# Single layer norms of a 16-sublayer kernel, rewritten: wide variance, Ln and Exp in place of Sqrt and reciprocal

## What is computed

```python
def _layernorm(x, axis=-1, eps=1e-05):
    m = jnp.mean(x, axis=axis, keepdims=True)
    v = jnp.var(x, axis=axis, keepdims=True)
    return (x - m) / jnp.sqrt(v + eps)
...
x = x + sublayer(_layernorm(x, axis=-1), weights)
```

## Time and profile before

| what | value |
| --- | --- |
| median of 3 runs | 3856.74 us (3844.39 to 3859.89) |
| the profiled execution | 3816.58 us, span 3814.8 us |
| TensorE (PE) busy | 3021.5 us, 79% |
| DVE (VectorE) busy | 2024.3 us, 53% |
| ACT (ScalarE) busy | 1374.9 us, 36% |
| GpSimd (POOL) busy | 670.1 us, 18% |
| mean granted TensorE clock | 0.864 |

### The profile page before, as it was taken

One profiled execution on the slowest core, in us unless ns is written; L12 is line 12 of the kernel. 1 busy time (PEld: TensorE's weight loads), 2 busy tenths in 40 slices (PEclk: granted clock), 3 DMA queues, 4 the chain that ended last, 5 costly groups with the idle time before them and its releaser, 6 DMA issues. The chain is left out here.

```text
span 3814.8 us, 57392 instructions
## 1 busy us (share of the span) xinstructions
PE 3021.5 (79%) x22522; PEld 1598.0 (42%) x22522; DVE 2024.3 (53%) x3730; ACT 1374.9 (36%) x2632; POOL 670.1 (18%) x561
## 2 busy tenths in 40 slices
PE   6566877788887699897688889977878658867986
PEld 4454247323475244444222224422233443654555
DVE  5211254588753788203788771166763453536643
ACT  3211434623243366423567762210102112223652
POOL 0000017065354100004443200000000000240003
PEclk9666869788888799999899999978789679977997
DMA  2022002022012321000311000000000000023202
GB/s 103 14 66 63 0 19 56 16 94 66 17 47 80 72 40 28 1 0 13 66 30 29 2 1 0 10 0 0 0 0 0 1 0 21 25 56 77 48 15 67
DMA packets 81292, 118.55 MB, mean 31 GB/s; under 512 B 12743, under 2 KB 51623, under 8 KB 79763
## 3 DMA queue, kind: packets, MB, share of 16 engines
q1 hardware_dynamic: 74003, 100.67, 10.6%
q0 software_dynamic: 7040, 14.43, 1.4%
HBM read 90.04 MB, written 24.81 MB: 30 GB/s over the span
## 5 line engine op out<-in xcount | busy, mean ns | idle before, releaser
L1674 DVE TENSOR_REDUCE at_mp<-PS 128x1 f32<-128x384 f32 (+3 forms) x640 | 313.3, 538 | 115.3 <-PE PS L1524 99.0
L1624 ACT ACTIVATE at_pt<-PS 128x384 f32<-128x384 f32 (+3 forms) x704 | 288.4, 456 | 212.8 <-PE PS L1536 177.6
L1521 PE MATMUL PS<-at_kx,at_qx 72*128 72x384 bf16 (+5 forms) x640 | 218.4, 346 | 67.7 <-DMA at_kx<-L_attn_a_parts 26.7
L1534 PE MATMUL PS<-at_qx,at_kx 105*128 105x512 bf16 (+5 forms) x704 | 214.8, 315 | 8.0 <-ACT at_pt L1624 6.0
L3860 ACT ACTIVATE ls_pt<-PS,ls_far 128x512 f32<-128x512 f32 x256 | 155.4, 684 | 23.1 <-PE PS L3681 18.6
L4007 DVE CUSTOM_DVE_ANT_0 PS<-PS,ls_pt 128x1024 f32<-128x1024 f32 x128 | 153.8, 1240 | 18.1 <-ACT ls_pt L3860 15.1
L2287 DVE TENSOR_TENSOR_SCAN mb_ring<-PS,mb_ring 128x1024 f32<-128x1024 f32 x64 | 146.6, 2291 | 18.9 <-POOL mb_ring L2226 6.7
L2242 PE MATMUL PS<-mb_ring,ident 128*128 128x512 f32 x256 | 147.7, 729 | 6.0 <-DVE mb_ring L2292 6.0
L1536 PE MATMUL PS<-at_above,identb 128*128 128x128 bf16 x704 | 134.1, 223 | 0.0
L2271 ACT ACTIVATE PS<-mb_dt,mb_a 128x1024 f32<-128x1024 f32 x64 | 71.6, 1118 | 168.1 <-DVE mb_ring L2287 168.1
L1521 PEld LDWEIGHTS PS<-at_kx,at_qx 102*128 102x128 bf16 (+1 forms) x640 | 64.5, 101 | 161.3 <-DVE at_mp L1674 85.6
(11 more groups left out here) (820 smaller groups left out, 6787.0 us busy)
## 6 DMA issues: line engine op xcount, KB each, us to landing
dl_arena<-in_fir_bank SPq DMA_DIRECT2D x32, 256.0 KB, 3.2
lnA<-mb_rows SPq DMA_DIRECT2D x16, 512.0 KB, 3.7
XN<-mb_rows SPq DMA_DIRECT2D x16, 512.0 KB, 3.7
ffn_place<-in_ffn_L SPq DMA_DIRECT2D x4, 1152.0 KB, 17.2
at_qx<-L_attn_a_parts SPq DMA_DIRECT2D x24, 192.0 KB
at_kx<-L_attn_a_parts SPq DMA_DIRECT2D x72, 64.0 KB
at_qx<-L_attn_b_parts SPq DMA_DIRECT2D x24, 192.0 KB
at_kx<-L_attn_b_parts SPq DMA_DIRECT2D x72, 64.0 KB
```

What stands on the lines that cost most here:

```text
L1521: mm = nc.tensor.matmul(PS[:, n % 3, 0:e - c], QX[0:RAW, u % 3, g, blk(i, P)], KX[0:RAW, u % 3, g, c:e], start=True, stop=True)
L1534: mm = nc.tensor.matmul(PS[:, 3 + n % 3, 0:e - c], KX[0:FULL, u % 3, g, blk(j, P)], QX[0:FULL, u % 3, g, c:e], start=True, stop=True)
L1624: nc.scalar.activation(PT[:, y % SLOTS, g, 0:e - c], PS[:, 3 + n % 3, 0:e - c], ACT.Exp, scale=SCALE).then_inc(exp_done, 1)
L1674: nc.vector.tensor_reduce(best, sc, AX.X, ALU.max).then_inc(s_maxed, 1)
```

## The change

The norm keeps each token's values on all partitions throughout. TensorE multiplies x by `center_mat` (identity less 1/128), which gives x less its mean straight into PSUM. ACT squares from PSUM into `lnA`. The variance product now has `mean_mat` stationary and 512 columns of squares moving, so every partition holds the variance. ACT takes Ln of variance plus eps, then Exp of minus a half times that, both 128x512, in place in `lnA` (`rstd` is now `lnA`). DVE does one product a block, from PSUM and `lnA` into `XN`. The narrow tile `rstd` is gone, and `center_mat` (64 KB) is built on GpSimd. The semaphores `mean_ready`, `std_ready`, `rstd_ready` and `spread_ready` go, `log_done` and `root_done` come.

```diff
-    sq, rstd = k.lnA, k.rstd
+    sq, rstd = k.lnA, k.lnA
...
         @block.tensor
         def _(pe):
+            def center(b):
+                nc.tensor.matmul(PS[:, b, :], k.center_mat[:, :], src[:, blk(b)], start=True, stop=True).then_inc(centered, 1)
+
             def variance(b):
                 pe.wait_ge(squared, b + 1)
-                for t in range(TB):
-                    mm = nc.tensor.matmul(PS[:, 4 + b, t:t + 1], sq[:, blk(TB * b + t, P)], k.mean_mat[:, 0:1], start=True, stop=True)
-                mm.then_inc(var_ready, 1)
-
-            def spread(b):
...
+                nc.tensor.matmul(PS[:, 4 + b, :], k.mean_mat[:, :], sq[:, blk(b)], start=True, stop=True).then_inc(var_ready, 1)
+
+            center(0)
+            center(1)
+            variance(0)
+            center(2)
+            variance(1)
+            center(3)
+            variance(2)
+            variance(3)
 
         @block.scalar
         def _(act):
             def square(b):
                 act.wait_ge(centered, b + 1)
-                nc.scalar.activation(sq[:, blk(b)], dst[:, blk(b)], ACT.Square).then_inc(squared, 1)
-
-            def deviation(b):
+                nc.scalar.activation(sq[:, blk(b)], PS[:, b, :], ACT.Square).then_inc(squared, 1)
+
+            def root(b):
                 act.wait_ge(var_ready, b + 1)
-                nc.scalar.activation(rstd[:, TB * b:TB * b + TB], PS[:, 4 + b, 0:TB], ACT.Sqrt, bias=k.eps_col[:, 0:1]).then_inc(std_ready, 1)
-
-            nc.scalar.activation(k.warm[:, 0:1], k.eps_col[:, 0:1], ACT.Sqrt)
+                nc.scalar.activation(rstd[:, blk(b)], PS[:, 4 + b, :], ACT.Ln, bias=k.eps_col[:, 0:1]).then_inc(log_done, 1)
+                act.wait_ge(log_done, b + 1)
+                nc.scalar.activation(rstd[:, blk(b)], rstd[:, blk(b)], ACT.Exp, scale=-0.5).then_inc(root_done, 1)
+
+            nc.scalar.activation(k.warm[:, 0:1], k.eps_col[:, 0:1], ACT.Ln)
             square(0)
-            for b in range(1, NBLK):
-                square(b)
-                deviation(b - 1)
-            deviation(NBLK - 1)
+            square(1)
+            for b in range(NBLK):
+                root(b)
+                if b + 2 < NBLK:
+                    square(b + 2)
...
         @block.vector
         def _(dve):
-            def center(b):
...
+            for b in range(NBLK):
+                dve.wait_ge(root_done, b + 1)
+                nc.vector.tensor_tensor(dst[:, blk(b)], PS[:, b, :], rstd[:, blk(b)], ALU.mult).then_inc(scaled, 1)
...
+            own(pool.memset(k.center_mat[:, :], -1.0 / D))
+            own(pool.affine_select(out=k.center_mat[:, :], in_=k.center_mat[:, :], compare_op=ALU.not_equal, fill=1.0 - 1.0 / D, base=0, pattern=[[-1, P]], channel_multiplier=1))
```

More of the change, by code:

```diff
@@ L105, in layernorm @@
     nc, PS = k.nc, k.PS
-    sq, rstd = k.lnA, k.rstd
-    TB = BLK // P
-    with stage(nc, "mean_ready", "centered", "squared", "var_ready", "std_ready", "rstd_ready", "spread_ready", "scaled", "pool_own") as (block, mean_ready, centered, squared, var_ready, std_ready, rstd_ready, spread_ready, scaled, pool_own):
+    sq, rstd = k.lnA, k.lnA
+    with stage(nc, "centered", "squared", "var_ready", "log_done", "root_done", "scaled", "pool_own") as (block, centered, squared, var_ready, log_done, root_done, scaled, pool_own):
         if beside is not None:
@@ L115, in _ @@
         def _(pe):
+            def center(b):
+                nc.tensor.matmul(PS[:, b, :], k.center_mat[:, :], src[:, blk(b)], start=True, stop=True).then_inc(centered, 1)
             def variance(b):
                 pe.wait_ge(squared, b + 1)
-                for t in range(TB):
-                    mm = nc.tensor.matmul(PS[:, 4 + b, t:t + 1], sq[:, blk(TB * b + t, P)], k.mean_mat[:, 0:1], start=True, stop=True)
-                mm.then_inc(var_ready, 1)
-            def spread(b):
[L123 to L129, removed]
-            variance(0)
-            for b in range(1, NBLK):
-                variance(b)
-                spread(b - 1)
-            spread(NBLK - 1)
+                nc.tensor.matmul(PS[:, 4 + b, :], k.mean_mat[:, :], sq[:, blk(b)], start=True, stop=True).then_inc(var_ready, 1)
+            center(0)
+            center(1)
+            variance(0)
+            center(2)
[3 more added lines that the diff above has]
+            variance(3)
         @block.scalar
@@ L4132, in constants @@
     k.ident = sb("ident", [P, P])
-    k.mean_mat = sb("mean_mat", [P, P])
+    k.mean_mat, k.center_mat = sb("mean_mat", [P, P]), sb("center_mat", [P, P])
     k.eps_col = sb("eps_col", [P, 1])
-    k.rstd = sb("rstd", [P, NTILE])
     k.rstd2 = sb("rstd2", [P, 2, NTILE])
```

## The result

| | before | changed |
| --- | --- | --- |
| median of 5 runs | 3856.74 us (3844.39 to 3859.89) | 3968.74 us (3965.0 to 3977.15) |
| ratio to before, 95% interval | | 1.0298 [1.0282, 1.0314] |
| profiled execution, span | 3814.8 us | 3963.3 us |
| mean granted TensorE clock | 0.864 | 0.844 |

The change makes the kernel 3.0% slower, 112.0 us by the medians. 3978 was predicted, with a range of 3940 to 4008.

What follows compares the result with a forecast made beforehand. TensorE bounds the calls before; ACT, with table loads on its path, after. Calls 105.9, GpSimd's lists -6.1, constants +0.7 and cold stages behind +21 sum to 121.5 us, added to the median 3856.7: 3978, range 3940 to 4008.

Steps and rivals of the forecast that it cites:

- The loads are on ACT's path: In each norm call, seven table loads between Ln and Exp cost 1.30 us each, 98 inside calls in all.
- Rival 1: In the norm calls, Ln and Exp need no load between them: 3845 us, not slower; chance 0.02.
- rival 2: In the norm calls, each switch costs another 1.3 us beyond its load: 127 us on top, 4105; chance 0.03.
- The sum of the calls: The 14 layernorm calls together get 105.9 us longer; a warm call goes from 11.54 to 19.85 us.
- the five calls counted as warm: Norm calls at a granted clock of 1.00 before: +8.3 us each.
- the seven: Norm calls at a granted clock of 0.81 to 0.87, lower at the start: +7.75 us each.
- the two by 8.9: Norm calls at a granted clock of 0.77, lower in the middle: 14.81 to 19.85 us, +5.05 each.
- The stage behind: Stages after the calls start at the lower TensorE clock, because TensorE idles at the call's end: +21 us.
- -6.1 for GpSimd: In two calls GpSimd's list already holds the closing barrier longer; the longer new call hides that: -6.1 us.
- Rival 3: Behind the calls the clock holds, so the last term is 0: 3957 us; chance 0.14.
- small products: Two stages behind calls begin with 32 small products in 3.71 us: 2 us more for each.
- Loads elsewhere: Outside the calls, the load at L1767 goes and one comes ahead of the copy at L2358: -2.6 and +2.6 us.

Runs made afterwards that it cites:

- e2: Changed kernel with Tanh in place of Ln and Exp for the warm-up, so no load inside a call (another norm computed): 3840.24 us, ratio 0.9960.
- e4: Changed kernel with ACT grouped by function and centrings ahead of variances, one load inside a call in place of seven: 3873.57 us, ratio 1.0047.
- e5: Kernel before with Ln and Exp in place of square root and reciprocal on the same narrow 128x4 tiles: 3939.96 us, ratio 1.0317.
- e9: Kernel before, unchanged, profiled once more on the same chip as the changed kernel: span 3858.8 us.
- e1: Kernel before, unchanged, profiled a second time: span 3852.7 us.
- the fillers: Changed kernel with 12 more products of 512 columns a call on TensorE, whose result nobody reads: 3945.7 us, ratio 1.0230.
- e10: Changed kernel profiled once more, beside before on one chip: span 3969.0 us, ratio 1.0308.
- the straight kernel: Changed kernel with Abs_reciprocal_sqrt in place of Ln and Exp, and four centrings first, then four variances: 3801.59 us, ratio 0.9953.

## Why the prediction was right

**The loads are on ACT's path, at 1.30 each.** Right, and shown three ways: taken away (e2), taken down to one (e4), and put alone on narrow tiles (e5). The 112 loads of 1283 ns were executed. Rival 1 (no load needed) and rival 2 (a switch costs more) are both out. The first is the rule of the Trainium skill (ScalarE: Activation LUTs, "Table sets: the hidden batching unit") that Ln followed by Exp is one load: here each of 98 switches had its own, and without them the kernel took 3840.24 us where rival 1 had put it at 3845. The 1.38 us of drain that the same page of the Trainium skill adds to a load ("What ACT_TABLE_LOAD costs") isn't in the rows: Ln ends at 1821.96, the load starts at 1821.97, Exp starts at 1823.27.

**The sum of the calls.** 105.9 us forecast; 103.0 by the first two profiles, 96.1 to 100.9 against the two later ones of before. In the four calls that start at full clock (4, 5, 8 and 12) 19.85 was forecast and 19.16 to 19.31 came. Two sizes were off. Ln 0 is at 3.0 and not 3.4, since ACT's first load starts 0.18 ahead of the first matmul, and square 0 runs from 1.22. And the chain from Ln 0 to the last Exp is 15.4 and not 15.7, since a square starts 0.1 before the Exp ahead of it has ended. The other calls came to 20.4 to 21.6. Part of the fit is luck: three of these ten (6, 11 and 13) had been counted as warm, at 19.85. They started at the lower clock and came to 20.4 to 21.6, which made up for the sizes: by the first two profiles the five calls counted as warm grew by 43.1 us (41.5 forecast), the seven by 51.0 (54.25), the two by 8.9 (10.1). What I didn't see is that a call has no fixed class. Calls 5, 6 and 13 ran at 1.00 in the first profile and took 1.7 to 2.9 us longer, partly at the lower clock, in e9. Call 11 ran at 1.00 in all three profiles of before and started at the lower clock in both of the changed kernel; why is open.

**The stage behind.** +21 forecast, -6.1 for GpSimd, +0.7 for constants: 15.6. Measured outside the calls: 9.6 (against e1) and 14.1 (against e9). Two profiles of the changed kernel differ by 7 us here outside the two stretches, so the size fits no better than that. The mechanism is shown by the fillers, at 19 us by the profiles. Rival 3 is out by the granted clock of 0.50 behind all 14 calls, and not by the total: 3968.74 lies 12 us from its 3957 and 9 from 3978. In the range the upper end takes 34 us for this term and leaves out the 4 us of the small products. It isn't spread as I had it, 1.7 us for each of ten. By e10 less e9, the stretch behind call 7 lost 6.1, behind call 5 4.4, behind 13 3.8, behind 6 3.5; those behind calls 3 and 9 lost -0.1 and 0.6, though their first 3 us are at 0.50 too. Of the two calls in which GpSimd's list is now covered, 4.7 us came back behind call 2, and nothing net behind call 4 (519.4 to 522.5).

**Loads elsewhere.** Forecast at +2.6 behind call 6 and -2.6 behind call 8: measured +3.5 and -4.1, with the clock in both. The two at L1624, gone too, the prediction leaves out. That these two, the five at L323, L560 and L2726 and the new one at L3501 cost nothing was not tried by itself.

**The base.** Adding the difference to the median, and not to the 3816.6 of the profiled execution, was right: 121.5 forecast, 112.0 measured. Had I trusted the profiled execution the forecast would have been 3938, just under the range. That it lay 40 us below the median had a cause of its own: the two stretches of level 0 that go with the set are 32 us of it (1177.6 less 1145.9).

## What to carry to other kernels

Before putting two activation functions in a loop, read the compiled order for table loads between them, and count those: here 98 loads of 1.30 us outweighed a third less work on TensorE (6.9 us for 10.8 a call at full clock) and half less on DVE. When a call is shortened or lengthened, ask who holds its barrier and what TensorE's clock does behind it; a long idle tail of TensorE costs the next stage (19 us over 14 calls here), and two spare products may be worth more than a better order (0.3% against nothing, with intervals that just touch). Compare profiles only from one chip and one set, and stage by stage.

## What the runs showed of the hardware

The same kernel took 3818.9 us on one chip and 3854.3 and 3852.8 on two others, with most of the difference (some 30 of 35 us) in two stretches of together 1150 us in level 0. These chips were used in one set each, so why, and whether it is the chip, stays open. Abs_reciprocal_sqrt takes 687 ns for 128x512 from PSUM with a bias column, as long as Ln. And TensorE's clock can be held with products that nobody reads: 12 a call moved the granted clock from 0.78 to 1.00 in a call of the same length (19.16 and 19.18 us), and 2 behind the last variance of the straight kernel were enough to have the first 3 us behind all 14 calls at 1.00.
